# Residual rows loaded ahead of a store, own buffers for one chunk, a reordered end and 41 unused products

## The reference

```python
# attention: 16 heads of 64; each block of 16 tokens sees token 0 and 5 blocks, masked causally
sim  = q @ k_window.T                    # 81 keys, of which the causal mask leaves the own block and two before it
attn = softmax(sim)
attn = einsum('gh,bhnij->bgnij', w_th, attn)   # mixes the heads
out  = (attn @ v_window) @ w_out + b_out       # the first token's row is its own v
x1   = layernorm(x + out)
# feed-forward with ternary weights, x / rms(x) at the entry of each product
h    = gelu(ternary_linear(x1, w_up))    # 128 -> 512
y    = ternary_linear(h, w_down)         # 512 -> 128
return layernorm(x1 + y)
```

## Time and profile before

| | us |
|---|---|
| median of 3 runs | 278.1 |
| lowest, highest | 276.99, 279.89 |
| the profiled execution, whole | 278.77 |
| its span in the profile | 276.2 |
| busy in the span: PE / DVE / ACT / POOL | 228.5 / 187.1 / 162.2 / 96.5 |

### The profile page before, as it was taken

The page is one execution under the profiler, slowest core; times in us unless marked ns, Lnnn a source line. Parts: engine busy times, 40 slices in busy tenths (PEclk is TensorE's granted clock), DMA queues, the critical chain, the costliest instruction groups (busy, mean ns, idle before and its releaser), DMA issues.

```text
span 276.2 us, 9860 instructions
## 1 busy us (share of the span) xinstructions
PE 228.5 (83%) x4258; PEld 204.3 (74%) x4258; DVE 187.1 (68%) x486; ACT 162.2 (59%) x306; POOL 96.5 (35%) x114
## 2 busy tenths in 40 slices
PE   1888988999999999989998999899987898428460
PEld 1787876778899898879887988898876787427450
DVE  0465588878676875688567856785778875176780
ACT  1475455666656569745975697569745268007541
POOL 6032432421332251535262625262536210055150
PEclk9999999999999999999999999999999799959855
DMA  7743640010020001001001100110010000100001
GB/s 230 214 116 97 225 101 2 13 50 0 5 58 3 21 13 52 0 25 52 9 1 42 51 12 0 44 41 21 0 43 2 0 4 2 39 19 2 0 29 49
DMA packets 18622, 11.67 MB, mean 42 GB/s; under 512 B 2004, under 2 KB 17940, under 8 KB 18452
## 3 DMA queue, kind: packets, MB, share of 16 engines
q1 hardware_dynamic: 17872, 9.94, 12.3%
q10 hardware_dynamic: 708, 1.12, 1.4%
HBM read 8.91 MB, written 2.10 MB: 40 GB/s over the span
## 4 chain that ended last, share of the span: by engine, by line
PE 44%; DVE 20%; ACT 18%; issue 12%; DMA 2%; POOL 1%; POOLq 0%; DVEq 0%; ACTq 0%
PE bank L1039 7%; PE bank L1041 6%; PE bank L1040 6%; PE bank L1158 5%; PE bank L1184 5%; DVE CTl L829 5%; ACT Yb L552 4%; ACT CTh L552 3%; DVE AT L834 2%; PE bank L1142 2%; DVE E L843 2%; DMA xq<-in_L_attn_x 2%; ACT L636 2%; PE bank L1254 2%; DVE mx L841 2%
## 5 line engine op out<-in xcount | busy, mean ns | idle before, releaser
L484 POOL TENSOR_TENSOR E<-E,rc 128x400 f32<-128x400 f32 x32 | 27.9, 872 | 83.7 <-DVE rc L851 83.6
L829 DVE TENSOR_TENSOR CTl<-bank,CTh 128x512 fp32r<-128x512 f32 x64 | 41.1, 685 | 22.2 <-ACT CTh L552 21.7
L552 ACT ACTIVATE Yb<-bank 128x512 f32<-128x512 f32 x64 | 38.3, 599 | 29.1 <-PE bank L1041 28.5
L1039 PE MATMUL bank<-xTh,Gh 128*128 128x256 f32 x128 | 39.8, 311 | 7.7 <-ACT Yb L552 6.4
L1039 PE MATMUL bank<-CTh,Mh 128*128 128x256 f32 x128 | 37.3, 292 | 4.0 <-DVE CTl L829 2.8
L680 ACT ACTIVATE E<-E 128x400 f32<-128x400 f32 x32 | 17.3, 539 | 39.2 <-DVE E L843 39.0
L552 ACT ACTIVATE CTh<-bank 128x512 fp32r<-128x512 f32 x64 | 34.7, 599 | 5.2 <-PE bank L1184 4.9
L1040 PE MATMUL bank<-CTl,Mh 128*128 128x256 f32 x128 | 36.3, 284 | 0.9 <-issue 0.9
L1041 PE MATMUL bank<-CTh,Ml 128*128 128x256 f32 x128 | 36.3, 284 | 0.0
L1040 PE MATMUL bank<-xTl,Gh 128*128 128x256 f32 x128 | 35.8, 280 | 0.0
L1041 PE MATMUL bank<-xTh,Gl 128*128 128x256 f32 x128 | 35.7, 279 | 0.0
(11 more groups left out here) (137 smaller groups left out, 477.8 us busy)
## 6 DMA issues: line engine op xcount, KB each, us to landing
raw<-in_L_attn_x SPq DMA_DIRECT2D x36, 64.0 KB
w_sb<-in_L_attn_w_qkv ACTq DMA_DIRECT2D x2, 512.0 KB, 5.7
pt_rows<-PT SPq DMA_DIRECT2D x1, 1024.0 KB, 5.6
R<-pt_rows SPq DMA_DIRECT2D x1, 1024.0 KB, 4.9
xr<-in_L_attn_x SPq DMA_DIRECT2D x6, 128.0 KB
out<-y SPq DMA_DIRECT2D x6, 128.0 KB, 2.3
raw<-in_L_attn_x SPq DMA_DIRECT2D x12, 56.0 KB
xq<-in_L_attn_x SPq DMA_DIRECT2D x2, 256.0 KB, 5.6
```

The lines of the kernel that those rows point to most:

```text
L484: tt(e, e, rc[s % 2][:, :].unsqueeze(2).broadcast_to([P, TILES, WIN]), ALU.mult).then_inc(s_norm, 1)
L552: copy = lambda o, i, **k: nc.scalar.activation(o, i, ACT.Copy, **k)
L829: v.tensor_tensor(ct_view(CTl[s // 4 % 2], s % 4, q), c_view(s, q), ct_view(f32(CTh[s // 4 % 2][:, :, :]), s % 4, q), ALU.subtract).then_i ...
L1039: mm(o, wh, rh, start=start, stop=False, **k)
```

## The change

- SyncE: the rows of chunks 6 and 7 are issued before store(3). The rows of chunk 7 no longer wait for residual(6): they go to the tile `raw`, which is free when GpSimd has split the last window (s_xwl), and have a semaphore of their own.
- Buffers: chunk 5 gets a third set of gT, gTh, gTl (`gset`: 5 is set 2, 6 is set 1, all others 0). The squares of chunks 4 to 6 go to gsq, those of chunk 7 to gT of set 2. gelu(5) waits for no other chunk; gelu(7) waits for the low part of chunk 4 only.
- In the loop: ScalarE makes `squares(n)` behind `down_out(n)` instead of before `y_out(s, 1)`; VectorE makes `result_shift(n)` behind `total` instead of first in the step.
- The end: the low parts of chunk 4 move from GpSimd to VectorE, the squares of chunk 5 from GpSimd to ScalarE. TensorE makes up(5) inside o_part(7) and down(5) before up(6). ScalarE and VectorE follow in a new order, which the diff shows. On GpSimd last_root(5) comes before hidden_root(6).
- TensorE: `keep_busy(bank, count)` issues products of wuT with itself, 128 rows by 256 columns, into a bank that nobody reads: 5, 4, 8, 12, 6 and 6, in all 41.

Left out of the diff below: the replacement of the buffer index `[n == 6]` by `[gset(n)]` in hidden_low, hidden_high, down and squares, and of `xr` and `s_xr` by their pairs in residual_rows and residual.

```diff
@@ -101,7 +101,7 @@
         raw = sb("raw", [P, CPAIR, P])
 
 
-        xr = sb("xr", [P, CT, P])
+        xr = [sb("xr", [P, CT, P]), raw[:, 0:CT, :]]
         attnS = sb("attnS", [P, CHUNK])
         res = [sb(f"res{i}", [P, CT, P]) for i in range(2)]
         x1n = sb("x1n", [P, CT, P])
@@ -138,9 +138,14 @@
             xq = pb("xq", [P, NT, P])
 
         with ExitStack() as last:
+            high5 = last.enter_context(nc.sbuf_tensor("gTh5", [P, FT, CHUNK], F32R))
+            low5 = last.enter_context(nc.sbuf_tensor("gTl5", [P, FT, CHUNK], F32R))
             gT.append(last.enter_context(nc.sbuf_tensor("gT6", [P, FT, CHUNK], F32)))
             gTh.append(last.enter_context(nc.sbuf_tensor("gTh6", [P, FT, CHUNK], F32R)))
             gTl.append(last.enter_context(nc.sbuf_tensor("gTl6", [P, FT, CHUNK], F32R)))
+            gT.append(last.enter_context(nc.sbuf_tensor("gT5", [P, FT, CHUNK], F32)))
+            gTh.append(high5)
+            gTl.append(low5)
             gsq = last.enter_context(nc.sbuf_tensor("gsq", [P, FT, CHUNK], F32))
             for n in range(6, 8):
                 res.append(last.enter_context(nc.sbuf_tensor(f"res{n}", [P, CT, P], F32)))
...
@@ -306,7 +311,10 @@
             return bank[(0, 2)[q] if s == 30 else C_BANK[q]]
 
         def squared(n):
-            return gT[0] if n < 4 else gsq
+            return gT[0] if n < 4 else gsq if n < 7 else gT[2]
+
+        def gset(n):
+            return {5: 2, 6: 1}.get(n, 0)
 
         def heads(i):
 
@@ -385,14 +393,17 @@
             flat = out.rearrange("b n c -> (b n) c")
 
             def residual_rows(n):
-                need(sp, f_res, n)
+                if n < CHUNKS - 1:
+                    need(sp, f_res, n)
+                else:
+                    sp.wait_ge(s_xwl, CHUNKS)
                 b, t0 = n // 4, 1 + n % 4 * CHUNK
                 if n % 4 < 3:
...
@@ -416,10 +427,9 @@
                     store(c - 5)
                 if c >= 3:
                     residual_rows(c - 2)
-            store(CHUNKS - 5)
             residual_rows(CHUNKS - 2)
             residual_rows(CHUNKS - 1)
-            for n in range(CHUNKS - 4, CHUNKS - 1):
+            for n in range(CHUNKS - 5, CHUNKS - 1):
                 store(n)
             n = CHUNKS - 1
             sp.wait_ge(f_out7, 1)
...
-
-            def squares(n):
-
-                pool.wait_ge(f_gelu, 2 * n + 2)
-                pool.wait_ge(f_ss, n)
-                for t in range(2):
-                    o = slice(2 * t, 2 * t + 2)
-                    tt(squared(n)[:, o, :], gT[n == 6][:, o, :], gT[n == 6][:, o, :], ALU.mult).then_inc(f_sum, 1)
 
             for s in range(STEPS):
                 for n, k in ffn(s):
@@ -534,15 +536,12 @@
                     rows_low(s // 4)
 
             variance_roots(6)
-            hidden_low(4, 0)
-            hidden_low(4, 1)
             variance_roots(7)
-            squares(5)
             hidden_root(4)
             last_root(4)
             hidden_root(5)
+            last_root(5)
             hidden_root(6)
-            last_root(5)
             hidden_root(7)
             last_root(6)
             last_root(7)
@@ -630,18 +629,17 @@
                 act.wait_ge(f_up, 2 * n + t + 1)
                 if n < 5:
                     need(act, f_ss, n)
-                elif n != 6:
-                    act.wait_ge(f_gl, 10 if n == 5 else 12)
-                    act.wait_ge(f_sum, 10 if n == 5 else 12)
-                nc.scalar.activation(gT[n == 6][:, 2 * t:2 * t + 2, :], up_bank(n, t)[:, :].rearrange("p (f c) -> p f c", f=2),
+                elif n == 7:
+                    act.wait_ge(f_gl, 10)
+                nc.scalar.activation(gT[gset(n)][:, 2 * t:2 * t + 2, :], up_bank(n, t)[:, :].rearrange("p (f c) -> p f c", f=2),
                                      ACT.Gelu).then_inc(f_gelu, 1)
 
             def hidden_high(n, t):
 
                 act.wait_ge(f_gelu, 2 * n + t + 1)
-                need(act, f_dn, {6: 0, 7: 6}.get(n, n))
+                need(act, f_dn, {5: 0, 6: 0, 7: 5}.get(n, n))
                 o = slice(2 * t, 2 * t + 2)
-                copy(gTh[n == 6][:, o, :], gT[n == 6][:, o, :]).then_inc(f_gh, 1)
+                copy(gTh[gset(n)][:, o, :], gT[gset(n)][:, o, :]).then_inc(f_gh, 1)
 
             def squares(n, t):
...
@@ -649,9 +647,11 @@
                 o = slice(2 * t, 2 * t + 2)
                 if n < 4:
                     act.wait_ge(f_gl, 2 * n + t + 1)
+                elif n < 7:
+                    act.wait_ge(f_ss, n)
                 else:
-                    act.wait_ge(f_ss, n)
-                nc.scalar.activation(squared(n)[:, o, :], gT[n == 6][:, o, :], ACT.Square).then_inc(f_sum, 1)
+                    act.wait_ge(f_gl, 12)
+                nc.scalar.activation(squared(n)[:, o, :], gT[gset(n)][:, o, :], ACT.Square).then_inc(f_sum, 1)
 
...
@@ -678,10 +678,6 @@
                 e = E[s % 2][:, :, 0:WIN]
                 act.wait_ge(s_sub, s + 1)
                 nc.scalar.activation(e, e, ACT.Exp).then_inc(s_exp, 1)
-                for n, k in ffn(s):
-                    if k == 4 and n < 4:
-                        squares(n, 0)
-                        squares(n, 1)
                 y_out(s, 1)
                 if s < len(IN_STEP):
                     fills(IN_STEP[s])
@@ -691,6 +687,8 @@
                 for n, k in ffn(s):
                     if k == 4 and n < 4:
                         down_out(n)
+                        squares(n, 0)
+                        squares(n, 1)
                     if k == 1:
                         x1_hi(n)
                     if k == 3 and n < 4:
@@ -715,24 +713,26 @@
             hidden_high(4, 1)
             squares(4, 0)
             squares(4, 1)
+            gelu(5, 0)
+            gelu(5, 1)
+            hidden_high(5, 0)
+            hidden_high(5, 1)
             result(3)
             stage(7)
-            gelu(5, 0)
             x1_hi(6)
-            gelu(5, 1)
             down_out(4)
-            hidden_high(5, 0)
-            hidden_high(5, 1)
             gelu(6, 0)
             gelu(6, 1)
+            down_out(5)
             x1_hi(7)
             hidden_high(6, 0)
             hidden_high(6, 1)
+            squares(5, 0)
+            squares(5, 1)
             gelu(7, 0)
             gelu(7, 1)
             hidden_high(7, 0)
             hidden_high(7, 1)
-            down_out(5)
             squares(6, 0)
...
@@ -954,8 +954,6 @@
             dve.wait_ge(s_eps, 1)
             for s in range(STEPS):
                 for n, k in ffn(s):
-                    if k == 7:
-                        result_shift(n)
                     if k == 2:
                         x1_lo(n)
                 if s == LAG + 1:
@@ -978,6 +976,8 @@
                 for n, k in ffn(s):
                     if k == 5:
                         second_sum(n)
+                    if k == 7:
+                        result_shift(n)
                 if s < len(IN_STEP):
                     fills(IN_STEP[s])
                 if s == 2:
@@ -998,29 +998,31 @@
             x1_lo(5)
             residual(6)
             layernorm(5)
+            hidden_low(4, 0)
+            hidden_low(4, 1)
             input_scale(6)
             up_input(6)
+            hidden_low(5, 0)
+            hidden_low(5, 1)
             residual(7)
             x1_lo(6)
             layernorm(6)
             input_scale(7)
             up_input(7)
-            hidden_low(5, 0)
-            hidden_low(5, 1)
             hidden_sum(4)
+            second_sum(4)
             x1_lo(7)
-            second_sum(4)
             hidden_low(6, 0)
             hidden_low(6, 1)
+            second_norm(4)
+            hidden_sum(5)
             layernorm(7)
+            second_sum(5)
             hidden_low(7, 0)
             hidden_low(7, 1)
-            second_norm(4)
-            hidden_sum(5)
-            second_sum(5)
-            hidden_sum(6)
             second_norm(5)
             result_shift(4)
+            hidden_sum(6)
             second_sum(6)
             hidden_sum(7)
...
@@ -1255,6 +1257,11 @@
                                      squared(n)[:, t, P * i + lo:P * i + lo + 32], ones[:, 0:1],
                                      start=(t == 0), stop=(t == FT - 1), skip_group_check=True)
                 ins.then_inc(f_ss, 1)
+
+            def keep_busy(bk, count):
+
+                for i in range(count):
+                    mm(bank[bk][:, 0:CHUNK], wuT[:, 0:P], wuT[:, 0:CHUNK], start=True, stop=True)
 
             def queries(s, b):
 
@@ -1310,28 +1317,34 @@
             o_part(6, 3)
             attn_back(6)
             o_part(7, 0)
+            up(5, 0)
+            up(5, 1)
             o_part(7, 1)
             o_part(7, 2)
             o_part(7, 3)
             x1_T(6)
+            keep_busy(6, 5)
             attn_back(7)
-            up(5, 0)
-            up(5, 1)
             down(4)
+            down(5)
+            keep_busy(6, 4)
             up(6, 0)
```

(36 more changed lines are left out.)

## The result

| | before | after |
|---|---|---|
| median, us | 278.6 (4 runs, 276.99 to 279.89) | 266.83 (4 runs, 266.46 to 267.62) |
| span of the profiled execution, us | 276.2 | 264.9 |
| granted clock over the span | 0.952 | 0.983 |

The ratio is 0.9584, with a 95% interval from 0.9527 to 0.9641: 4.2% faster; the medians differ by 11.8 us. The forecast was 267.4 us.

The account below looks back on a forecast made before the run. Bound: the attention loop with TensorE busy, then a last 60 us where chunk 6's load waits behind store(3). Gains 8.6 + 1.1 + 1.0 = 10.7 us take the profiled 278.8 to 268.1, as median 267.4 us; range 265.3 to 271.3.

Parts of the forecast that it names:

- The signs that it names: Expected in the new trace, among them residual(6) near 230, no DMA wait of VectorE, some 4 us wait before L907.
- the walk: Last stretch, followed in 8 steps from attn_back(6) to result(7) at 261.25 instead of 269.88: 8.6 us gained.
- The old bound: Last stretch: residual(6) idles 8.76 us for chunk 6's load, which SyncE's queue holds behind store(3).
- Two terms of 1.1 and 1.0 us: Loop: squares behind down_out give 1.1 us (bounds 0 and 1.6), result_shift later in its step 1.0 (0 and 2.0).
- 3 x 0.4: Loop: three of TensorE's four waits for the Yb copy count as gain, 1.1 us with the shorter ones' 0.35.
- the wait of hidden_low(5) for down(4): Last stretch, step 3: VectorE stands 4.2 us before hidden_low(5), which asks for down(4) although its buffers are its own.
- In the walk they delay a used product by 0.1 us at most: Last stretch: the 41 idle products, 4.9 us of TensorE, lie where it waits and never delay a product on the road.
- Their good is in it: Last stretch: the walk takes 2.4 GHz throughout, so the idle products' benefit is already counted; called the least certain term.
- The rival of the clock: Last stretch: TensorE's clock falls in spite of the idle products, costing some 3 us, 270.4 us; chance 0.15.
- The load still late: Rival: chunk 6's load stays late because SyncE stands elsewhere; 278 less the loop's 2.1, 276 us; chance 0.02.
- The overlap of 2.1 us: Last stretch: GpSimd's subtraction of chunk 4 over two tiny VectorE instructions put 2.1 us on the path; now gone.
- The clash that the prediction fears for the new order: Near 234: GpSimd's roots(6) against VectorE's hidden_low(4), some 0.5 us by the port-lock rule, falling in the 4.2 us wait.

Follow-up runs that it names:

- e5: The kernel before with one edit: the rows of chunks 6 and 7 issued ahead of store(3); 269.42 us, ratio to before 0.9647.
- e4: The changed kernel with store(3) issued before the rows of chunks 6 and 7 again; 278.86 us, ratio to before 1.003.
- e9: The kernel before with three edits: rows ahead of store(3), squares behind down_out, result_shift behind total; 268.07 us, ratio to before 0.9594.
- e1: The changed kernel with the squares of chunks 0 to 3 made again before the last Yb copy of their chunk; 268.12 us.
- e3: The changed kernel without the 41 products that nobody uses; 268.04 us, ratio to before 0.9595.
- e6: The kernel before with the two edits of the loop: squares behind down_out, result_shift behind total; 275.86 us, ratio to before 0.9893.
- e2: The changed kernel with result_shift made first in its step again; 267.57 us.

## Why the prediction was right, step by step

**The number.** Forecast were 267.4 us and a range from 265.3 to 271.3, measured 266.83. In the profile the forecast gain was 10.7 us (8.6 in the last stretch, 2.1 in the loop), measured from the mark 11.27 (8.51 and 2.76). The signs that it names are there: residual(6) at 229.29 without a wait for a DMA, one wait of 4.27 us before L907, no wait for Yb in the loop, TensorE's hole near 213 at 1.86 us, 20.4 us from hidden_low(5) to result(7), and L875 at 0.34.

**The load and the walk.** The old bound and its cause in SyncE's queue were right: moving the store alone gives 8.66 us (e5), and putting it back takes everything (e4). The load for chunk 6 is issued at 216.3; with the 4.1 us that it took before it lands 9 us ahead of its use, as predicted. The walk gave 29.50 us from attn_back(6) (231.75) to result(7) (261.25); measured were 228.82 to 258.48, 29.66. Its intermediate points hold too: hidden_low(5) 9.20 us behind attn_back(6) against 9.25, second_sum(6)'s start 24.75 against 24.96. That the whole last stretch comes out at the gain of the load alone was no merit of the walk's separate parts: the new order's gain and the wait that it brings cancel (e9).

**The loop.** Two terms of 1.1 and 1.0 us; measured 1.44 and 1.32, together 2.76 against 2.1. For result_shift the place and the size at step 30 were right (0.97 against 0.9), and 0.35 us go with the clock. For the squares the step that failed is "3 x 0.4", the wait alone as the gain of each chunk: against the kernel before the gains are 1.25, 0.16 and 0.03, against e5 0.85, 0.32 and 0.29, against e1 0.64, 0.44 and 0.17. In each row the first is the largest and above its wait of 0.36 us, since the pause at square_sum goes with it (e1). At the later ones TensorE, coming sooner, met waits for x1n and x1_lo of VectorE, 0.9 and 0.5 us in all in the view of waits up to 230, where before there was one, of 0.3; that they ate the rest is argued, no run takes them away. The sum was nearly right over wrong parts, which is luck.

**Own buffers, new order.** I put them into the walk and never walked without them. The prediction names the wait of hidden_low(5) for down(4) and calls the buffers its own, but doesn't draw the conclusion that this wait gives back what the buffers bring. e5 and e9 show that the old order reaches result(7) just as soon: from step 31 it takes them 38.66 and 38.11 us, the changed kernel 38.84.

**Idle products.** "In the walk they delay a used product by 0.1 us at most" held nearly: the six before down(7) end at 251.7, its last input comes at 251.35, and the 0.3 us aren't on the road. "Their good is in it" was 0.56 us. The rival of the clock did not come about: the products held it. Its price of 3 us is not tested, since it counted 12 idle products at half clock, 2.5 us, which e3 doesn't have. What e3 does show is that half clock over TensorE's last 9.6 us (246.7 to 256.3) costs the used work 0.56 us.

**The load still late.** This rival was priced at 276, the old time less the loop's gain. In e4 it is 278.9: under a late load the new order is worse than the old one with the same loop (155.6 against e6's 153.1 from the mark). attn_back(7) and down(4) stand behind x1_T(6) in both orders; two other things are new. ScalarE now makes gelu(5) and hidden_high(5) ahead of result(3), so that store(3), and the load behind it, are issued 2.25 us later (121.77 against 119.52 from the mark) and residual(6) starts 3.0 later. And hidden_low(5), which waits for down(4), stands ahead of residual(7), which starts 5.5 us later than in e6. The new order wins 3.0 us back behind that.

**The share of GpSimd.** The overlap of 2.1 us is gone, but e5, which keeps it, loses at most 0.2 us by it: its x1_T(6) comes late by the overlap, at 238.47, and attn_back(7) behind it at 238.74, but stage(7), on which attn_back(7) waits as well, ends only at 238.53. The overlap was on the chain of waits of before and off the road, but for this, once the load was early. The clash that the prediction fears for the new order, roots(6) against hidden_low(4), at some 0.5 us, doesn't show in the changed kernel: the two overlap by 0.7 us, GpSimd's roots take 1.03 us (1.01 elsewhere) and VectorE's pair 1.28, as always.

```profile
230.88 1.03 POOL L500 TENSOR_TENSOR roots<-var_in,exps 128x4 f32<-128x4 f32 x1 [8.31 <-DVE var_in L870]
...
231.22 1.28 DVE L907 TENSOR_TENSOR gTl<-gT,gTh 128x512 fp32r<-128x512 f32 x2
```

## What to carry to other kernels

Look first at what stands in front of a load in its own queue: a store that waits for results holds up every load behind it, and moving it gave here 8.7 of 11.3 us; with two small edits in the loop it gave as much as the whole change with its rewritten end. Before crediting an edit with its part of a walk, walk once without it; and when a tile gets its own buffer, take out the waits that guarded the shared one, or it may bring nothing, as here. Idle products that keep TensorE's clock are on the road as soon as the inputs behind them come sooner, so they have to be counted again after each improvement.

## What the runs showed of the hardware

- A wait of TensorE of 0.36 us ahead of 64 small products goes with a pause of 0.7 to 1.3 us some 3 us later, at the end of the next 64 small ones, for which no semaphore is named. With the wait gone the pauses shrink from 3.8 us in four to 0.8 in two. The pauses of two kernels with the same loop (before and e5) differ by up to 0.4 us one by one and by 0.1 in sum; what sets the size of one is open.
- The granted clock fell behind a hole of 2.8 us in the kernel before and in e5, not in e2; behind one of 1.8 to 1.9 us it fell in e1, e6 and e9, not in the changed kernel. Half clock over the 12 products behind it cost the step 0.35 us (6.15 against 5.80), a later fall nothing.
- Two VectorE operations on 128x1 took 2.43 and 2.49 us (before, e5) under a GpSimd operation on 128x512 and 0.34 us without it; a VectorE subtraction of 128x512 that overlapped GpSimd's operation on 128x4 took no longer than alone.
- The start of the same code, up to step 15, took 113.6 to 115.8 us in fourteen profiled executions of these kernels, and the rest of the changed kernel, the one that was profiled twice, repeated to 0.01 us. For differences under 1 us a mark behind the start tells more than the whole time, as long as the granted clock over the stretch is held against it.
